# A loop of semaphore additions on SyncE beside the two hop stages of a graph kernel

## The reference

```python
for _ in range(K):                                    # K = 2
    x = jax.ops.segment_sum(x[src] * norm, dst, num_segments=n)
```

## Time and profile before

| | us |
|---|---|
| median of 3 runs | 27719.22 |
| lowest and highest | 27716.97, 27924.35 |
| the profiled execution, whole | 27758.51 |
| its span, first to last instruction | 27756.8 |
| hop 0, first to last start of a gather | 13077.52 to 17681.44 |
| hop 1, the same | 17744.54 to 22353.89 |

### The profile page before, as it was taken

The page is one execution under the profiler, slowest core; times in us unless marked ns, Lnnn a source line. Parts: engine busy times, 40 slices in busy tenths (PEclk is TensorE's granted clock), DMA queues, the critical chain, the costliest instruction groups (busy, mean ns, idle before and its releaser), DMA issues. The chain is left out here.

```text
span 27756.8 us, 312901 instructions
## 1 busy us (share of the span) xinstructions
PE 13056.3 (47%) x63827; PEld 12457.6 (45%) x63828; DVE 11400.3 (41%) x24717; ACT 5617.9 (20%) x17566; POOL 16913.9 (61%) x16986
## 2 busy tenths in 40 slices
PE   0333333333333338997333333333333368888887
PEld 0233322333333338996333333333333357777777
DVE  2377711111111117775111111111111179999999
ACT  6422221100000002221000000000000035555554
POOL 1677766456666660001666666666666668888887
PEclk8555555555555558887555555555555578888888
DMA  1111111222222221110000000200000022222223
GB/s 47 14 15 15 15 14 14 12 54 58 58 59 58 58 58 29 30 30 21 12 11 12 12 11 11 13 12 12 12 11 11 11 36 43 43 43 43 43 43 41
DMA packets 2490687, 794.43 MB, mean 29 GB/s; under 512 B 1958608, under 2 KB 2281393, under 8 KB 2489651
## 3 DMA queue, kind: packets, MB, share of 16 engines
q0 software_dynamic: 517120, 331.99, 8.9%
q1 hardware_dynamic: 1623714, 242.33, 5.3%
q10 hardware_dynamic: 349748, 219.11, 3.1%
HBM read 699.49 MB, written 93.71 MB: 29 GB/s over the span
## 5 line engine op out<-in xcount | busy, mean ns | idle before, releaser
L990 POOL DMA_INDIRECT hop_far<-hop_rows,hop_index x6464 | 6113.6, 946 | 5816.4 <-issue 4739.0
L1026 PE MATMUL hop_total<-hop_far,hop_hot 128*128 128x32 f32 x12928 | 3019.3, 378 | 6228.5 <-issue 3426.9
L1026 PEld LDWEIGHTS hop_total<-hop_far,hop_hot 128*128 128x128 f32 x12928 | 2973.7, 323 | 6275.5 <-issue 6274.1
L773 POOL DMA_INDIRECT weighted_far<-in_x_dram,weighted_rows x3232 | 3342.4, 1034 | 1973.1 <-issue 1031.2
L1005 DVE TENSOR_TENSOR hop_hot<-hop_iota,local_of_edge 128x512 f32<-128x512 f32 x1616 | 1057.9, 687 | 8119.2 <-DMA rows_by_src<-push_row,push_index 6369.5
L1098 POOL DMA_INDIRECT rows_by_src<-push_row,push_index x3232 | 3103.9, 960 | 1705.3 <-issue 1586.4
L2123 POOL DMA_INDIRECT conv_far<-conv_rows x3232 | 3322.2, 1028 | 964.6 <-issue 865.1
L1148 PE MATMUL push_near<-far_rows_sb,push_turned 128*128 x6464 | 1636.0, 434 | 3166.8 <-issue 2344.3
L857 PE MATMUL weighted_total<-weighted_message,weighted_hot 128*128 128x33 f32 x6464 | 1514.6, 404 | 3345.6 <-issue 2050.8
L2229 PE MATMUL conv_radial_a<-radial,conv_hidden 128*128 128x256 f32 x6464 | 2737.5, 511 | 640.7 <-DVE conv_products_b L2361 564.9
L1148 PEld LDWEIGHTS push_near<-far_rows_sb,push_turned 128*128 128x128 f32 x6464 | 1553.4, 328 | 3249.4 <-issue 3247.8
(11 more groups left out here) (256 smaller groups left out, 20609.0 us busy)
## 6 DMA issues: line engine op xcount, KB each, us to landing
push_line<-local_by_group ACTq DMA_DIRECT2D x808, 256.0 KB
hop_far<-hop_rows,hop_index POOLq DMA_INDIRECT x6464
conv_weights<-weight_by_group SPq DMA_DIRECT2D x808, 128.0 KB
att_far<-rows_by_src SPq DMA_DIRECT2D x880, 80.0 KB
weighted_far<-in_x_dram,weighted_rows POOLq DMA_INDIRECT x3232
push_place<-place_by_dst SPq DMA_DIRECT2D x3232, 0.5 KB
rows_by_src<-push_row,push_index POOLq DMA_INDIRECT x3232
conv_rows<-edges_by_dst SPq DMA_DIRECT2D x3232, 4.0 KB
```

The lines of the kernel that those rows point to most:

```text
L773: pool.indirect_dma_start(far[s][:, j, :], None, table, bass.IndirectOffsetOnAxis(ap=rows[s][:, j, 0:1].bitcast(I32), axis=0)).then_inc(ga ...
L990: pool.indirect_dma_start(far[s][:, j, :], None, table, bass.IndirectOffsetOnAxis(ap=index[s][:, j:j + 1], axis=0)).then_inc(gathered[s], 16)
L1026: last = pe.matmul(total[:].rearrange("p n c -> p (n c)")[:, bass.ds(at[s % SLOTS * HALVES + j // COLUMNS] * F, F)], hot[s][:, j, :], far[ ...
```

## The change

Each hop gets a block for SP. It is a loop over the 101 passes; in each it clears a semaphore of its own, `stepped`, and then for each of the eight groups waits until that group's rows are gathered (the condition that PE waits for) and adds 1 to `stepped` 24 times. Nobody waits for `stepped`. As built, a pass is 197 instructions on SP: 192 additions, of which the first of each group carries the wait, and five for the loop and the clearing. PE, DVE, ACT and POOL keep the same instructions in the same order; in the program only line numbers differ there (by 1 from line 653 on, by 11 behind line 969).

```diff
+STEPS = 24
...
         closed = k.sem(f"{name}_closed")
+        stepped = k.sem(f"{name}_stepped")
         block = ctx.enter_context(nc.Block())
+
+        @block.sync
+        def _(sp):
+            with loop(sp, 0, PASSES) as i:
+                sp.sem_clear(stepped)
+                for s in range(DEEP):
+                    sp.wait_ge(gathered[s], (i + 1) * (16 * PER))
+                    for _ in range(STEPS):
+                        sp.sem_inc(stepped, 1)
```

## The result

| | us |
|---|---|
| kernel before, median of 4 runs | 27808.02 (27716.97 to 27924.35) |
| changed kernel, median of 4 runs | 29346.28 (29245.19 to 29425.29) |
| ratio of the times, 95% interval | 1.0541 (1.0503 to 1.0579) |
| the profiled execution of the changed kernel | 29277.62 |

A forecast was written before the change was run, and what follows sets the result against it. Bound: POOL's gather pace plus PE's holds not covered by eight buffers. Profiled 27758.5 us less 1075 gives 26,683; less 39 for standing above the median, 26,650 us, 3.9% faster; range 26,560 to 28,200.

The forecast's parts named there:

- The bound: In the hops: POOL's pace, 5.00 us per group of four gathers, plus the part of PE's holds eight buffers don't cover.
- PE's holds: In the hops: PE starts one matmul every 2.8 us with nothing to wait for; excess 1131 us for both hops.
- The cost of an addition: SP in the hops: 0.057 us each, 24 are 1.4 us of a group's 5.00 us; cost on the path 0.
- The wait, and the fetch: SP's loop: waiting for gathered rows costs 0; a loop's repeat fetches nothing, otherwise SP alone pays, with 3.6 us slack.
- Who is held, and when: Across stages: holds belong to stages with few instructions, and where SP has a stream, SP is held and PE goes free.
- I take 95% of it, 1075 us: Hops: the gain taken from the 1131 us of excess, since not every excess gap of POOL need come from PE.
- the sign that I took for it: Push stage: PE's matmuls have a maximum of 452 ns against a median of 434, read as PE not held.
- Rival 3: Hops: each added instruction adds to what causes holds, PE is held more; up to +1270 us, 28,990; chance 0.15.
- Rival 4: Hops: SP is held as in the push stage, and all wait for it at a hop's end; 34,300 us; chance 0.10.
- Its two prices: SP held in hops: 0.34 us more per instruction, +3.3 ms per hop; or 68% of the time, and SP keeps up.
- it keeps up: SP in a hop: 1.6 us free in each 5.00 give room for 28 instructions, and it needs 25.
- Cover: End of a hop: 12 us before the barrier hide a late SP; it comes onto the path only beyond that.

The follow-up runs named there:

- A set without holds: Third set, another chip: the kernel before, no edit, 25442.38 us (31 runs); its hop 1 lasts 4032.9 us, 3231 steps of 1.248.
- the pass of 390 instructions: SP's loop in the changed kernel with 48 additions per group instead of 24: 32354.21 us, ratio 1.1616.
- the first set of experiments: Changed kernel with 8 additions (ratio 1.002), 48 (1.1616) or no wait (29185.09 us); kernel before with 24 on DVE (1.0458); kernel before 27901.46 us.
- the three later sets: Second, third and fourth sets of runs, each beside the unedited kernel before, at 25420.01, 25442.38 and 25444.12 us.
- The first two sets of experiments: Sets with the kernel before, no edit, at 27901.46 us in the first and 25420.01 us in the second.
- the four kernels made for the question: Kernel before plus 24 additions on ACT (1.0024) or 8 on DVE (1.0); changed kernel with one of four matmuls (25427.85 us) or gathers (20059.99 us).
- another kernel of 16%: Changed kernel with 48 additions per group instead of 24: 32354.21 us, ratio 1.1616 in the first set; ratio 1.002 in the third.

## Why the prediction was wrong, point by point

**The bound: right.** POOL's pace and what PE's holds cost were read rightly. A set without holds ran at POOL's pace to 0.2%, and the excess that the holds had cost, 1131 us by the prediction, was 1135.

**The cost of an addition: right as a duration, wrong as a pace.** 0.057 us was read from eight additions in a row; behind the hops they pass at 0.062. In the hop they pass at 0.64, and that is where they are. The earlier trace rows lie just ahead of a dense stage, and I took their price into a stage in which my own reading said that engines are held. The sum put the additions at 0 on the path; they measured 738 + 735 = 1473 us, nearly all of the loss.

**The wait, and the fetch: right for this loop.** Without the wait the tail stands; the queue moved four packets more. The general form, that a loop's repeat fetches nothing, does not hold: the pass of 390 instructions moved 1004 packets more than the one of 197.

**The step that failed is "Who is held, and when",** and with it the choice in the sum, "I take 95% of it, 1075 us". It inferred from the push stage that with a stream on SP "it is SP that is held and PE goes free". SP was held, and PE as well, in the same stretches and for more time than before (4361.8 us against 3426.9): the two hops are 106 us longer and not 1075 shorter. The push stage didn't show a trade, only a PE that went through its groups whole. And the sign that I took for it, a longest matmul of 452 ns against a median of 434, tells nothing: in the hops, where the holds are, PE's own line in the trace of before reads

```profile
L1026 PE MATMUL hop_total<-hop_far,hop_hot x12928: 209/401/420, 13083.8 to 22375.3; 128*128 128x32 f32 x199
```

Its longest matmul is 19 ns above the median there too; PE's holds lie between its matmuls. On DVE a trade was seen, to no profit.

**Rival 3, "PE held more": seen, and hardly at a price.** PE's held time is 935 us longer. With 8 additions, with 48 and without SP's wait it is 868, 969 and 1014 us longer (4294.4, 4395.7 and 4441.2 us), so it doesn't grow with the number of instructions as the rival has it; of before with the holds there is only one trace to compare with. The hops' 106 us are within what unchanged stages vary by.

**Rival 4, "SP last", came true,** at 0.10, and so did its picture: POOL and PE finish, and all wait for SP. They don't finish early, though; the hops are no shorter. Its two prices bracket the time. By the price per instruction, held from first to last, +3.3 ms per hop; by the share of time, nothing. What happened is neither: 0.64 us per instruction in the hop, more than its 0.40, and then 0.062 as soon as the others stop, since the holds end when their work does. A hop thus costs the backlog at the fast pace, 0.74 ms. The way to "it keeps up" was the error: it took the 68% lost in the push stage as a share of time, which makes an addition of 0.057 us one of 0.18, and 28 against 25 seemed room enough. The other reading of the same rows, so much per instruction, was nearer, and even the plainest one was: three instructions in 1.48 us are 0.49 us each, 11 or 12 in a group's 5.7 us, so some 9400 of the 19,897 in a hop. The 10,500 left over are 0.60 ms at 0.057 us, and the sum is 27,720 + 1200 = 28,900 us. Only that the backlog would pass at the fast pace was not to be seen in the trace of before, which has no stretch with SP alone at work; with the slow pace kept to the end it is the rival's 34,300, and both would have been bounds. The range, which ended at 28,200, left rival 4 out whole.

**Cover.** "A late SP comes onto the path only beyond" 12 us was right, and the eight additions show the other side of it: 8.6 instructions per group fit in, and cost nothing that the times can tell (ratio 1.002, 0.9994 to 1.0046).

**What stays open.** What the holds are. They hit SP in the push stage and the hops, PE in the hops, ACT in the weighted sum (its semaphore instructions of line 877, median 17 ns, up to 1396 ns) and DVE where it had the additions; those of SP and PE share a step of about 0.70 us; and they ended when the other engines stopped. The runs on record with the prediction and the first set of experiments have them, the three later sets don't. The first two sets of experiments name the same chip, about 20 minutes apart, so it isn't a fixed property of that chip; what differed between them I can't tell. Who is held where several engines have work is not settled either: beside SP's stream PE is held too, beside DVE's it is not in the stretches shown, and the four kernels made for the question met no holds. Whether recording the profile has a part in it can't be told, for every run here has its span and clock on record. The Trainium skill, in NOTIFIC — the notification-queue block, section 10 (Constraints, capacities, measured rates), has it that a record costs an engine no cycles; no row here shows one, and no run here was made to test it.

## What to carry to other kernels

An engine "that is idle there" is free only if it keeps up at the pace that the stage really gives it, and that pace is read from the same kind of stage as (instructions started) / (time), not from one instruction's duration. What it can't do in time is paid behind the stage, at the barrier, where the whole backlog is run off. The longest instruction of an engine doesn't tell whether it is held either, if the holds lie between its instructions. Where a profile shows maxima fifty times the median on register moves and semaphore additions, first run the kernel before again: here 9% of its time came and went with no edit, and an effect of 5%, in another kernel of 16%, with it. Compare kernels only within one set that runs the kernel before too, and look in it for such maxima before any verdict.

## What the hardware showed that I had not expected

- Holds of sequencer instructions come and go with no change of program: SP's additions, median 17 ns, have a maximum of 1449 ns in one set and of 17 ns in another, with the kernel before at 27901.46 us in one and 25420.01 in the next, on a chip of the same number.
- Two engines are held at once, by one step: in one stretch SP's additions last up to 1395 ns, with a median of 691, and PE's matmuls start 2.11, 2.79 and 2.80 us apart, all near to multiples of 0.70 us.
- They depend on the others' work: the same loop passes at 0.64 us per addition beside the hop and at 0.062 us as soon as PE, DVE, ACT, POOL and the DMA engines are still.
- 24 additions per group on DVE or ACT, engines of the ring itself, cost nothing where nothing is held (ratios of 1.002 and 1.0024): DVE has 5.00 us for each group and is busy for 0.69 of them.
- A loop on SP with 197 instructions is fetched once (4 packets more on the instruction queue), one with 390 at each turn (1096 packets against 92), and an addition in it takes 0.070 us instead of 0.062.
